# Edges laid out on 126 partitions instead of 128 in a two-layer graph kernel

## The chip, the cores and the metric

The kernel runs on one core of a Trainium2 chip. The time is device time in microseconds (us) of one execution; a kernel's time is the median of its executions. TensorE (PE), VectorE (DVE), ScalarE (ACT), GpSimd (POOL) and SyncE (SP) each run their own stream of instructions and meet at semaphores. 16 DMA engines move data between HBM and SBUF; plain transfers are asked for by SP, transfers whose rows are picked by a list of indices (indirect DMAs) by POOL.

## The reference

6,250 nodes with 256 features go through two layers; each has a graph part, a mixing part and a feed-forward part. The graph has 200,000 edges. `dst` is sorted, `src` is random, and every edge has 128 attributes. What the change touches is the first graph part and what the edges are prepared for:

```python
edge_index = jnp.stack([src, dst])
in_deg = jnp.minimum(jax.ops.segment_sum(ones, dst, num_segments=num_nodes), MAX_IN_DEGREE - 1)
out_deg = jnp.minimum(jax.ops.segment_sum(ones, src, num_segments=num_nodes), MAX_OUT_DEGREE - 1)
edge_proj = edge_attr @ W_sum + b_sum
sum3d = jax.ops.segment_sum(edge_proj, src, num_segments=num_nodes)
return x + z_in[in_deg] + z_out[out_deg] + cent_term + vor_term + sum3d
```

The second layer's graph part gathers `x[src]` and sums it by `dst`. So the edge attributes have to be brought together by `src`, and the pairs (src, dst) are wanted by `dst`.

## The kernel before, in words

Nodes are taken in 50 blocks (`NT`) of 125 (`P`). The block of an edge is `hi`, its place in the block is `lo`. Edges lie on `Q` = 128 partitions: partition p holds the `EF` = 1562 consecutive edges from p * EF on, in `EF` columns, and the `TAIL` = 64 edges that are left lie one on a partition in column EF. Columns are filled up to `EC` = 1568, a multiple of 32; the other slots hold pads. Every DVE and ACT instruction on edges works on [Q, EC], or on [Q, n columns].

The program is a row of blocks with a barrier after each.

**The first block** (lines 302 to 441). SP loads `src` and `dst`, DVE makes `hi` and `lo` (lines 400 to 407), and then the edges of each of the 50 blocks are counted: DVE counts the first 20 (`count_block`, line 200), ACT gets the other 30 from 31 sums of signs (line 427). Short matmuls (lines 253 to 263) turn the counts into the first place of every partition's edges of each block (`first_src`).

**The second block** (lines 463 to 893) holds the scatter. Columns go in halves of `HC` = 16. SP loads the attributes of a half, [128 partitions x 16 columns x 128 numbers], into one of the two halves of `ring` (`load`, line 535) as soon as the scatters of 16 columns out of that half have landed. POOL prepares a half with two small copies (`stage_half`, lines 568 and 569: the key into `ring`, the places into `stage`), and then issues one indirect DMA for each column (`scatter_half`, line 576): each takes one row of 516 bytes from each of the Q partitions and writes it to its place in `rows_by_src`. The two copies for the next half stand before the last three scatters of a half. There are EF + 1 scatters, 1563.

The places come from `rank_chunk` on DVE, for four chunks of columns (`CHUNKS`, in units of 32 columns: 0 to 6, 6 to 20, 20 to 34, 34 to EC/32). In each, the 50 blocks pass through a mask (line 621), a scan (627) and a predicated copy (634). POOL waits for the first chunk before its first scatter, and for each later one before it prepares that chunk's first half (`next_chunk`). After the ranks DVE counts `dst` in the same way (line 200, 50 instructions), and then makes one-hot tiles of 8 columns for `src` and then for `dst` (lines 605 and 608, EC/8 tiles for each), from which PE counts degrees (line 808). Layer statistics, the sigmoid terms and the attention-like mixing follow on DVE, ACT and PE; they need nothing of the scatter.

**After it** a short block writes `pairs_by_dst` in one direct copy, since `dst` is sorted; the next block (from line 1004 on) reads `rows_by_src` in windows of 1024 rows, and the rest of the program does not depend on Q.

Of the kernel before, what the change touches and what calls it, by code (L numbers as in the profile page):

```python
# [22 lines left out]
N, D, E, ED = 6250, 256, 200000, 128  # L23
P = 125
NT = N // P
Q = 128
EF = E // Q
TAIL = E - Q * EF
EC = -(-(EF + 1) // 32) * 32
# [57 lines left out]
def program(nc, a, out):  # L87
# [102 lines left out]
    def sort_dve(dve, ch, tools, hi, width, tab_b, tab_s, first2, base=None, signs=None):  # L190

        mask, cnt, tot, first, col, col_i, cum, row, win_f, ps, counted, summed = tools
        shift = width.bit_length() - 1
        nw = tab_b.shape[1]
        block_counted = sem("block_counted")

        def count_block(b, u):
            if not isinstance(b, int) or b >= 2:
                at(dve, block_counted, b - 1, passed["dve"])
            dve.tensor_scalar(mask[:, u * EC:(u + 1) * EC], hi[:], iota_f[:, bass.ds(b, 1)], 0.0,  # L200
                              ALU.is_equal, ALU.add, accum_out=cnt[:, bass.ds(b, 1)]).then_inc(block_counted, 1)

        for b in range(2):
            count_block(b, b)
        counted_here = SIGN_FROM if signs else NT
        with dve.Fori(1, counted_here // 2) as i:
            for u in range(2):
                count_block(i * 2 + u, u)
        dve.wait_ge(block_counted, counted_here)
        if signs:  # L210
            sums, signs_summed = signs
            rest = cnt[:, SIGN_FROM:NT]
            dve.wait_ge(signs_summed, NT + 1 - SIGN_FROM)
            ch.step(dve.tensor_tensor(rest, sums[:, SIGN_FROM:NT], sums[:, SIGN_FROM + 1:NT + 1], ALU.subtract))
            ch.step(dve.tensor_scalar(rest, rest, 0.5, None, ALU.mult))
        ch.step(dve.tensor_copy(tot[:], cnt[:]))
        dve.sem_inc(counted)
        dve.wait_ge(summed, 1)

        ch.step(dve.tensor_copy(tot[:], ps[:, 0, 64:64 + NT]))  # L220
        ch.step(dve.tensor_tensor_scan(first[:], tot[:], tot[:], 0.0, ALU.add, ALU.bypass))
        ch.step(dve.tensor_tensor(first2[:], first[:], tot[:], ALU.subtract))
        ch.step(dve.tensor_tensor(first[:], first2[:], ps[:, 0, 0:NT], ALU.add))
        ch.step(dve.tensor_scalar(first2[:], first[:], -1.0, None, ALU.add))

        ch.step(dve.tensor_copy(col[0:NT, 0:1], ps[0:NT, 0, 128:129]))
        ch.step(dve.tensor_scalar(col_i[0:NT, 0:1], col[0:NT, 0:1], float(width - 1), None, ALU.add))
        ch.step(dve.tensor_scalar(col_i[0:NT, 1:2], col_i[0:NT, 0:1], shift, None, ALU.arith_shift_right))
        ch.step(dve.tensor_copy(col[0:NT, 1:2], col_i[0:NT, 1:2]))
        ch.step(dve.scalar_tensor_tensor(out=col[0:NT, 2:3], in0=col[0:NT, 1:2], scalar=-float(width),  # L230
                                         in1=col[0:NT, 0:1], op0=ALU.mult, op1=ALU.add))
        dve.sem_inc(counted)
        dve.wait_ge(summed, 2)
        ch.step(dve.tensor_copy(col[0:NT, 3:4], ps[0:NT, 0, 129:130]))
        ch.step(dve.tensor_scalar(cum[0:NT, 0:nw], win_f[0:NT, 0:nw], col[0:NT, 3:4], None, ALU.is_ge))
# [12 lines left out]
    def sort_pe(pe, tools, nw):  # L248
# [1 line left out]
        mask, cnt, tot, first, col, col_i, cum, row, win_f, ps, counted, summed = tools  # L250
        h = nw // 2
        pe.wait_ge(counted, 1)
        pe.matmul(ps[:, 0, 0:NT], lower[:], cnt[:], start=True, stop=True)  # L253
        pe.matmul(ps[:, 0, 64:64 + NT], ones[:], cnt[:], start=True, stop=True)
        pe.matmul(ps[0:NT, 0, 128:129], cnt[:], ones[:, 0:1], start=True, stop=True).then_inc(summed, 1)
        pe.wait_ge(counted, 2)
        pe.matmul(ps[0:NT, 0, 129:130], lower[0:NT, 0:NT], col[0:NT, 1:2], start=True, stop=False)
        pe.matmul(ps[0:NT, 0, 129:130], ident[0:NT, 0:NT], col[0:NT, 1:2], start=False, stop=True).then_inc(summed, 1)
# [7 lines left out]
    def rank_edges(dve, ch, hi, before, mask, rank, pos_f, pos):  # L266

        with dve.Fori(0, NT // 2) as i:
            ch.enter(i, 6)
            for u in range(2):  # L270
                b = i * 2 + u
                m = mask[:, u * EC:(u + 1) * EC]
                ch.step(dve.tensor_scalar(m, hi[:], iota_f[:, bass.ds(b, 1)], None, ALU.is_equal))
                ch.step(dve.tensor_tensor_scan(rank[:], m, m, before[:, bass.ds(b, 1)], ALU.add, ALU.bypass))
                ch.step(dve.copy_predicated(pos_f[:], m.bitcast(U16), rank[:]))
            ch.leave(NT // 2)
# [10 lines left out]
    win1_base = sbuf(s12, "win1_base", [128, NW1])  # L287
    z_idx = sbuf(s12, "z_idx", [128, NT * 2], I32)
    win_f = XT[:, 4 * EC:4 * EC + NW2]
    pos_f = XT[:, 2 * EC:3 * EC]  # L290
    s01 = ExitStack()
    pair = sbuf(s01, "pair", [Q, EC * 2], I32)
    pos_src = sbuf(s01, "pos_src", [Q, EC], I32)
# [8 lines left out]
    with ExitStack() as ctx:  # L302
        src_i = sbuf(ctx, "src_i", [Q, EC], I32)
        dst_i = sbuf(ctx, "dst_i", [Q, EC], I32)
        src_f = XT[:, 0 * EC:1 * EC]
        dst_f = XT[:, 1 * EC:2 * EC]
        rank = XT[:, 3 * EC:4 * EC]
        mask = sbuf(ctx, "mask", [Q, 2 * EC], BF16)
        signs = sbuf(ctx, "signs", [Q, 2 * EC], BF16)
        sign_sums = sbuf(ctx, "sign_sums", [Q, 64])  # L310
# [110 lines left out]
        def _(act):  # L421
            act.wait_ge(hi_ready, 1)

            def sum_signs(b, u):
                if not isinstance(b, int) or b >= SIGN_FROM + 2:
                    at(act, signs_summed, b - SIGN_FROM - 1, passed["act"])
                act.activation(signs[:, u * EC:(u + 1) * EC], hi_src[:], ACT.Sign, bias=above[:, bass.ds(b, 1)],
                               accum_out=sign_sums[:, bass.ds(b, 1)]).then_inc(signs_summed, 1)

            for u in range(2):  # L430
# [6 lines left out]
        @block.tensor  # L437
        def _(pe):
            pe.wait_ge(falls_ready, 1)
            pe.matmul(ps[0:1, 3, 0:1], falls[:, 3:4], ones[:, 0:1], start=True, stop=True).then_inc(falls_summed, 1)  # L440
            sort_pe(pe, src_tools, NW1)


# [25 lines left out]
    with ExitStack() as ctx:  # L469
# [28 lines left out]
        pqkv = psum(ctx, "pqkv", 4)  # L498
        pq, pkv = pqkv[:, 0:2, :], pqkv[:, 2:4, :]

        dst_tools = (XT[:, 5 * EC:6 * EC].bitcast(BF16), sbuf(ctx, "d_cnt", [Q, NT]), sbuf(ctx, "d_tot", [Q, NT]),
                     sbuf(ctx, "d_first", [Q, NT]), sbuf(ctx, "d_col", [64, 8]), sbuf(ctx, "d_col_i", [64, 2], I32),
                     XT[:, 0:NW2], XT[0:1, NW2:2 * NW2], win_f, pqkv, sem("d_counted"), sem("d_summed"))
        ptr = psum(ctx, "ptr", 2)
# [1 line left out]
        phist = psum(ctx, "phist", 1)  # L506
        numbers = pctx[:, 0, 0:128]
        CHUNKS = ((0, 6), (6, 20), (20, 34), (34, EC // (2 * HC)))
        masks = XT[:, 6 * EC:7 * EC].bitcast(BF16).rearrange("p (m c) -> p m c", m=4)

        weights_in, mix_w_in, v_ones = sem("weights_in"), sem("mix_w_in"), sem("v_ones")
        ring_in = [sem("ring_in0"), sem("ring_in1")]
# [85 lines left out]
        def _(dve):  # L598
            ch = chain("dve", dve)

            def onehots(lo, hi, which):
                def body(t, u, i):
                    if later(t) or which:
                        at(dve, counted_to, t - 1 + which * (EC // 8), passed["dve"])
                    dve.tensor_tensor(lo1[:, u * 8 * P:(u + 1) * 8 * P].rearrange("p (c n) -> p c n", c=8),  # L605
                                      numbers[:, 0:P].unsqueeze(1).to_broadcast([Q, 8, P]),
                                      lo[:, bass.ds(t * 8, 8)].unsqueeze(2).to_broadcast([Q, 8, P]), ALU.is_equal)
                    dve.tensor_tensor(hi1[:, u * 8 * NT:(u + 1) * 8 * NT].rearrange("p (c n) -> p c n", c=8),  # L608
                                      numbers[:, 0:NT].unsqueeze(1).to_broadcast([Q, 8, NT]),
                                      hi[:, bass.ds(t * 8, 8)].unsqueeze(2).to_broadcast([Q, 8, NT]), ALU.is_equal).then_inc(onehot_ready, 1)  # L610
                tiles(dve, body, n=EC // 8)

            def rank_chunk(k):
# [16 lines left out]
                def place_block(b, u):  # L630
                    at(dve, scanned, b + (base + 1), passed["dve"])
                    if not isinstance(b, int) or base + b > 0:
                        at(dve, placed, b + base, passed["dve"])
                    dve.copy_predicated(out, masks[:, u, 0:n].bitcast(U16), pqkv[:, u, 0:n]).then_inc(placed, 1)
                    dve.tensor_copy(first_src[:, bass.ds(b, 1)], pqkv[:, u, n - 1:n]).then_inc(carried, 1)

                def block(b, u):
                    if not isinstance(b, int) or b < NT - 2:
# [262 lines left out]
    with s01, ExitStack() as ctx:  # L901
        pos_dst = sbuf(ctx, "pos_dst", [Q, EC], I32)
        mask = sbuf(ctx, "mask2", [Q, 2 * EC], BF16)
        rank, pos_f = XT[:, 0:EC], XT[:, EC:2 * EC]
        stage = sbuf(ctx, "stage2", [Q, 2 * 8], I32)
        pstage = sbuf(ctx, "pstage", [Q, 2 * 16], I32)
        pair_out = [sem("pair_out0"), sem("pair_out1")]
# [1445 lines left out]
```

## Time and profile before

| | us |
|---|---|
| median of 3 runs | 9076.64 (9044.06 to 9086.92) |
| the profiled execution, its own time | 9050.52 |
| its span | 9048.8 |

| engine | busy us of the span |
|---|---|
| PE | 3955.3 |
| PE weight loads | 3030.6 |
| DVE | 3517.7 |
| ACT | 719.5 |
| POOL | 3686.9 |

No engine is busy for half of the span, because the program is a row of stages with a different engine in front in each. A table by stretches of time says more than the totals: it shows in which stretch an engine works, and what the others do meanwhile. The rows are in the section before the prediction. Times of day are us from the start of the span. "issue" in a row is idle time for which the profile shows no other engine; "remote" is idle time that ended by a semaphore event that the profile can't put down to an instruction.

### The profile page before, as it was taken

Reading aid. Unit: us, or ns where it says so; the run is one execution under the profiler, and the core shown is the slowest. Engines: PE = TensorE matmul, PEld = TensorE weight load, DVE = VectorE, ACT = ScalarE, POOL = GpSimd, SP = SyncE. Lnnn points to the kernel's source line nnn. Section 1 sums busy time; section 2 is a strip of 40 time slices with the busy share of each in tenths; the row PEclk is TensorE's granted clock in tenths of the full one; section 3 lists DMA queues with packets and bytes.
Section 4 is the critical chain, followed back from the end, with each engine's and each line's share of the span. In section 5 each row is a group of like instructions: output and inputs, shape, how many; then the busy total and the mean of one; then the engine's idle time right before and its main releaser. Section 6 shows DMA issues by size and latency. Waiting matters only on the chain. (4 is left out here: it accounts for less than half of the span.)

```text
span 9048.8 us, 90350 instructions
## 1 busy us (share of the span) xinstructions
PE 3955.3 (44%) x18034; PEld 3030.6 (33%) x18035; DVE 3517.7 (39%) x7213; ACT 719.5 (8%) x1718; POOL 3686.9 (41%) x3922
## 2 busy tenths in 40 slices
PE   0000000000366366299378455565555555642792
PEld 0000000000355254199267233333333334432672
DVE  6321213200599722488622233333333333354112
ACT  2000000000000222000112000000000000221220
POOL 3576676677200000083000466666666663003104
PEclk9999999999999997599689566666667666875896
DMA  3233333333100000098000233333333334011113
GB/s 96 74 94 93 93 94 93 93 97 96 32 0 0 0 0 0 0 325 307 24 0 2 79 87 87 90 89 86 91 85 87 87 89 52 4 42 46 65 63 103
DMA packets 382516, 666.41 MB, mean 74 GB/s; under 512 B 207747, under 2 KB 236119, under 8 KB 369799
## 3 DMA queue, kind: packets, MB, share of 16 engines
q0 software_dynamic: 148768, 375.57, 14.0%
q1 hardware_dynamic: 233703, 290.37, 11.0%
q8 instruction: 13, 0.21, 0.0%
q14 instruction: 32, 0.26, 0.0%
HBM read 519.41 MB, written 146.21 MB: 74 GB/s over the span
## 5 line engine op out<-in xcount | busy, mean ns | idle before, releaser
L1496 POOL DMA_INDIRECT rows<-xn_rows,pw_in x1664 | 1624.2, 976 | 886.1 <-issue 484.7
L1629 PE MATMUL pg<-rows,hot 128*125 128x256 f32 x3328 | 1278.0, 536 | 1146.0 <-issue 401.1
L576 POOL DMA_INDIRECT rows_by_src<-ring,stage x1563 | 1499.7, 960 | 656.7 <-issue 488.8
L1629 PEld LDWEIGHTS pg<-rows,hot 128*125 128x125 f32 x3328 | 818.9, 265 | 1593.5 <-issue 1456.2
L1514 DVE TENSOR_TENSOR agg<-agg,pg 125x256 f32 x832 | 348.2, 419 | 1247.8 <-remote 544.2
L808 PE MATMUL phist<-hi,lo 128*125 128x50 bf16 x3136 | 413.6, 281 | 867.0 <-DVE hi L608 573.5
L253 PE MATMUL pqkv<-d_cnt,lower 128*128 128x50 f32 x2 | 0.7, 435 | 1578.5 <-remote 1578.5
L808 PEld LDWEIGHTS phist<-hi,lo 128*125 128x125 bf16 x3136 | 370.3, 222 | 911.6 <-issue 904.7
L1004 POOL MEMSET acc<- 128x6375 f32 x1 | 5.4, 5410 | 1493.0 <-POOLq L99 1493.0
L253 PEld LDWEIGHTS pqkv<-d_cnt,lower 128*128 128x128 f32 x2 | 0.5, 310 | 1579.0 <-remote 1579.0
L1095 PE MATMUL pw<-hot,win 128*128 128x125 f32 x3968 | 454.2, 277 | 164.1 <-DVE hot L1048 162.7
L1095 PEld LDWEIGHTS pw<-hot,win 128*128 128x128 f32 x3968 | 449.1, 193 | 169.8 <-issue 168.8
L1555 DVE TENSOR_TENSOR hot<-ids,pw_in 128x250 f32<-128x250 int32 x832 | 344.6, 414 | 385.9 <-issue 355.7
L605 DVE TENSOR_TENSOR lo<-pctx,lo_src 128x1000 bf16<-128x1000 f32 x196 | 232.8, 1188 | 629.3 <-remote 506.8
L627 DVE TENSOR_TENSOR_SCAN pqkv<-XT,first_src,pctx 128x448 f32<-128x448 bf16 (+2 forms) x200 | 206.9, 1034 | 485.6 <-issue 485.4
L1048 DVE SCALAR_TENSOR_TENSOR hot<-win,win_base,iota_f 128x1000 f32<-128x1000 f32 x248 | 338.5, 1365 | 26.1 <-POOL acc L1004 17.1
L964 POOL IOTA ids<- 128x6375 int16 x1 | 5.5, 5453 | 702.4 <-POOLq L1372 702.4
L183 ACT ACTIVATE rstd<-rstd 125x50 f32<-125x50 f32 x5 | 1.2, 245 | 3010.6 <-DVE rstd L176 3010.6
L605 DVE TENSOR_TENSOR lo<-pctx,lo_dst 128x1000 bf16<-128x1000 f32 x196 | 233.9, 1193 | 0.0
L2251 PE MATMUL e_py<-e_w,XT 128*128 x896 | 208.1, 385 | 45.1 <-ACT XT L2237 45.1
L2013 POOL MEMSET XT<- 32x12800 f32 x1 | 10.8, 10759 | 524.6 <-POOLq L99 524.6
L2198 POOL DMA_DIRECT2D moe_results<-XT x56 | 34.1, 610 | 456.1 <-DVE XT L2214 456.1
(413 smaller groups left out, 6424.6 us busy)
## 6 DMA issues: line engine op xcount, KB each, us to landing
win<-rows_by_src SPq DMA_DIRECT2D x248, 516.0 KB
ring<-in_edge_attr SPq DMA_DIRECT2D x97, 1024.0 KB
rows<-xn_rows,pw_in POOLq DMA_INDIRECT x1664
rows_by_src<-ring,stage POOLq DMA_INDIRECT x1563
XT<-moe_rows SPq DMA_DIRECT2D x56, 256.0 KB
moe_results<-XT POOLq DMA_DIRECT2D x56, 256.0 KB, 2.3
pw_in<-pairs_by_dst SPq DMA_DIRECT2D x832, 2.0 KB
e_w<-in_L_ffn_W SPq DMA_DIRECT2D x16, 512.0 KB
```

What stands on the lines that cost most here:

```text
L576: pool.indirect_dma_start(rows_d, bass.IndirectOffsetOnAxis(ap=stage[:, h * HC + j:h * HC + j + 1].bitcast(U32), axis=0), ring4[:, h, j, : ...
L605: dve.tensor_tensor(lo1[:, u * 8 * P:(u + 1) * 8 * P].rearrange("p (c n) -> p c n", c=8), numbers[:, 0:P].unsqueeze(1).to_broadcast([Q, 8, ...
L627: dve.tensor_tensor_scan(pqkv[:, u, 0:n], masks[:, u, 0:n], pctx[:, 0, 0:n], first_src[:, bass.ds(b, 1)], ALU.add, ALU.bypass).then_inc(sc ...
L808: mm = pe.matmul(phist[0:P, 0, which * 64:which * 64 + NT], lo1[:, (u * 8 + j) * P:(u * 8 + j + 1) * P], hi1[:, (u * 8 + j) * NT:(u * 8 + ...
L1048: dve.scalar_tensor_tensor(out=hot[:, (s % 4) * R1 * P:(s % 4 + 1) * R1 * P].rearrange("p (r n) -> p r n", r=R1), in0=keys.unsqueeze(2).to ...
L1095: mm = pe.matmul(pw[:, s % 4, 0:P], win[:, s * RC + r * (ED + 1):s * RC + r * (ED + 1) + ED], hot[:, ((s % 4) * R1 + r) * P:((s % 4) * R1 ...
L1496: pool.indirect_dma_start(rows[:, (2 * (s % RU) + r) * D:(2 * (s % RU) + r + 1) * D], None, xn2_d, bass.IndirectOffsetOnAxis(ap=pw_in[:, s ...
L1514: dve.tensor_tensor(tile, tile, pg[0:P, bank, 0:D], ALU.add).then_inc(acc_done, 1)
L1555: dve.tensor_tensor(hot[:, (s % 4) * 2 * P:(s % 4 + 1) * 2 * P].rearrange("p (r n) -> p r n", r=2), ids[:, bass.ds(b[s + early] * P, P)].u ...
L1629: mm = pe.matmul(pg[0:P, s % 4, 0:D], hot[:, ((s % 4) * 2 + r) * P:((s % 4) * 2 + r + 1) * P], rows[:, (2 * (s % RU) + r) * D:(2 * (s % RU ...
L2198: pool.dma_start(moe_y_d[bass.ds(t * MW, MW), :].rearrange("(p r) c -> p (r c)", p=128), yw[:, u * 2 * D:(u + 1) * 2 * D]).then_inc(y_out[ ...
L2251: mm = pe.matmul(py[:, v, 0:D], hT[:, (u * NH + m) * MW + v * 128:(u * NH + m) * MW + (v + 1) * 128], w2[:, bass.ds((e * NH + m) * D, D)], ...
```

## The change

`Q` becomes 126. `EF` is then 1587, `TAIL` 38, `EC` 1600 and the number of pad columns 13 instead of 6. Partition p holds edges 1587p and on. Tables that were [128, ...] and are used beside edges are cut to their first 126 partitions. Nothing changes its place in the program, but some counts follow from Q:

| | before | after |
|---|---|---|
| indirect scatters (EF + 1) | 1563 of 128 rows | 1588 of 126 rows |
| halves (of 16 columns, the last one shorter) | 98 | 100 |
| columns in the last chunk of ranks | 480 | 512 |
| columns in an instruction over all edges | 1568 | 1600 |
| one-hot tiles, `src` and `dst` | 392 | 400 |

```diff
-Q = 128
+Q = 126
...
-            dve.tensor_scalar(mask[:, u * EC:(u + 1) * EC], hi[:], iota_f[:, bass.ds(b, 1)], 0.0,
+            dve.tensor_scalar(mask[:, u * EC:(u + 1) * EC], hi[:], iota_f[0:Q, bass.ds(b, 1)], 0.0,
...
-        pe.matmul(ps[:, 0, 0:NT], lower[:], cnt[:], start=True, stop=True)
-        pe.matmul(ps[:, 0, 64:64 + NT], ones[:], cnt[:], start=True, stop=True)
-        pe.matmul(ps[0:NT, 0, 128:129], cnt[:], ones[:, 0:1], start=True, stop=True).then_inc(summed, 1)
+        pe.matmul(ps[0:Q, 0, 0:NT], lower[0:Q, 0:Q], cnt[:], start=True, stop=True)
+        pe.matmul(ps[0:Q, 0, 64:64 + NT], ones[0:Q, 0:Q], cnt[:], start=True, stop=True)
+        pe.matmul(ps[0:NT, 0, 128:129], cnt[:], ones[0:Q, 0:1], start=True, stop=True).then_inc(summed, 1)
...
-    pos_f = XT[:, 2 * EC:3 * EC]
+    pos_f = XT[0:Q, 2 * EC:3 * EC]
...
-                                      numbers[:, 0:P].unsqueeze(1).to_broadcast([Q, 8, P]),
+                                      numbers[0:Q, 0:P].unsqueeze(1).to_broadcast([Q, 8, P]),
...
-                    dve.tensor_tensor_scan(pqkv[:, u, 0:n], masks[:, u, 0:n], pctx[:, 0, 0:n], first_src[:, bass.ds(b, 1)],
+                    dve.tensor_tensor_scan(pqkv[0:Q, u, 0:n], masks[:, u, 0:n], pctx[0:Q, 0, 0:n], first_src[:, bass.ds(b, 1)],
```

The other edits of the diff cut `XT`, `iota_f`, `above`, `ones`, `numbers` and `ps` to 0:Q in the same way.

## Rows read from the trace of the kernel before

**Rows 1.** The page: totals of engines, busy tenths in 40 slices, chain that ended last.

```profile
PE 3955.3 (44%) x18034; PEld 3030.6 (33%) x18035; DVE 3517.7 (39%) x7213; ACT 719.5 (8%) x1718; POOL 3686.9 (41%) x3922
...
DVE  6321213200599722488622233333333333354112
...
POOL 3576676677200000083000466666666663003104
...
issue 1%; DVEq 0%; POOL 0%; DVE 0%; DMA 0%; PEldq 0%
```

**Rows 2.** Stretches of time: busy us (and instructions) of each engine, clock, DMA share.

```profile
core 0: us, PE busy (x) PEld busy (x) DVE busy (x) ACT busy (x) POOL busy (x), PEclk, DMA share, GB/s
...
1750.00:2000.00 250.00, 13.26 (x104) 12.05 (x104) 21.83 (x26) 0.00 (x0) 172.37 (x199) 1.00 0.31 93
...
2370.00:2500.00 130.00, 83.46 (x657) 75.84 (x657) 130.00 (x165) 0.00 (x0) 0.00 (x0) 1.00 0.00 0
```

**Rows 3.** Groups of POOL instructions, start to 2370 us: busy, mean ns | idle before.

```profile
L576 POOL DMA_INDIRECT rows_by_src<-ring,stage x1563 | 1499.7, 960 | 656.7 <-issue 488.8 <-remote 165.7 <-POOL stage L569 1.8
...
L568 POOL CAST ring<-pair 128x16 f32<-128x16 int32 x7 | 1.8, 257 | 100.5 <-DVE pos_src L656 100.5
```

**Rows 4.** POOL in order of time: start, duration, operation, idle before. Two halves.

```profile
602.88 0.96 POOL L576 DMA_INDIRECT rows_by_src<-ring,stage  x1 [0.31 <-issue]
604.14 0.96 POOL L576 DMA_INDIRECT rows_by_src<-ring,stage  x1 [0.30 <-issue]
605.10 0.23 POOL L568 CAST ring<-pair 128x16 f32 x1
605.24 0.20 POOL L569 COPY stage<-pos_src 128x16 int32 x1
605.61 0.98 POOL L576 DMA_INDIRECT rows_by_src<-ring,stage  x1 [0.16 <-issue]
606.89 0.95 POOL L576 DMA_INDIRECT rows_by_src<-ring,stage  x1 [0.30 <-issue]
608.14 0.96 POOL L576 DMA_INDIRECT rows_by_src<-ring,stage  x1 [0.30 <-issue]
615.07 0.96 POOL L576 DMA_INDIRECT rows_by_src<-ring,stage  x1 [5.96 <-remote]
```

**Rows 5.** POOL before chunk 1 of the ranks, in order of time.

```profile
384.22 0.96 POOL L576 DMA_INDIRECT rows_by_src<-ring,stage  x1 [0.30 <-issue]
433.03 0.36 POOL L568 CAST ring<-pair 128x16 f32<-128x16 int32 x1 [47.84 <-DVE pos_src L656]
```

**Rows 6.** Groups of POOL's DMAs in the whole span, shapes apart.

```profile
L1496 POOL DMA_INDIRECT rows<-xn_rows,pw_in x1664 | 1624.2, 976 | 886.1 <-issue 484.7 <-remote 152.2 <-PE pg L1629 146.8
...
L2022 POOL DMA_INDIRECT moe_rows<-XT,e_pos_x x100 | 98.0, 980 | 176.1 <-DVEq L2104 145.9 <-issue 30.2
...
L2198 POOL DMA_DIRECT2D moe_results<-XT x56 | 34.1, 610 | 456.1 <-DVE XT L2214 456.1
```

**Rows 7.** DMA queues from 600 to 2300 us (packets, MB, share), and issues.

```profile
q1 hardware_dynamic: 10800, 78.65, 16.7%
q0 software_dynamic: 38624, 79.80, 14.7%
...
ring<-in_edge_attr SPq DMA_DIRECT2D x75, 1024.0 KB
rows_by_src<-ring,stage POOLq DMA_INDIRECT x1208
```

**Rows 8.** Line 605: duration min/median/max, first and last start.

```profile
L605 DVE TENSOR_TENSOR lo<-pctx,lo_src x196: 1185/1185/1200, 1677.9 to 2619.9; 128x1000 bf16<-128x1000 f32 x196
L605 DVE TENSOR_TENSOR lo<-pctx,lo_dst x196: 1185/1190/1200, 2621.5 to 2937.3; 128x1000 bf16<-128x1000 f32 x196
```

**Rows 9.** DVE in order of time as the scatter ends.

```profile
2367.53 1.20 DVE L605 TENSOR_TENSOR lo<-pctx,lo_src 128x1000 bf16<-128x1000 f32 x1 [17.24 <-remote]
2368.64 0.56 DVE L608 TENSOR_TENSOR hi<-pctx,hi_src 128x400 bf16<-128x400 f32 x1
2369.12 1.19 DVE L605 TENSOR_TENSOR lo<-pctx,lo_src 128x1000 bf16<-128x1000 f32 x1
```

**Rows 10.** Groups of all engines, 120 to 2370 us.

```profile
L605 DVE TENSOR_TENSOR lo<-pctx,lo_src 128x1000 bf16<-128x1000 f32 x38 | 45.5, 1199 | 629.3 <-remote 506.8 <-issue 122.5
```

**Rows 11.** Groups of all engines from the start to 147 us.

```profile
L427 ACT ACTIVATE signs<-hi_src,above 128x1568 bf16<-128x1568 bf16 x31 | 49.1, 1588 | 10.7 <-DVEq L406 10.7
...
L200 DVE TENSOR_SCALAR_CACHE_REDUCE mask<-hi_src,iota_f 128x1568 bf16<-128x1568 bf16 x20 | 35.4, 1844 | 0.0
```

More of the change, by code:

```diff
@@ L218, in sort_dve @@
         dve.wait_ge(summed, 1)
-        ch.step(dve.tensor_copy(tot[:], ps[:, 0, 64:64 + NT]))
+        ch.step(dve.tensor_copy(tot[:], ps[0:Q, 0, 64:64 + NT]))
         ch.step(dve.tensor_tensor_scan(first[:], tot[:], tot[:], 0.0, ALU.add, ALU.bypass))
         ch.step(dve.tensor_tensor(first2[:], first[:], tot[:], ALU.subtract))
-        ch.step(dve.tensor_tensor(first[:], first2[:], ps[:, 0, 0:NT], ALU.add))
+        ch.step(dve.tensor_tensor(first[:], first2[:], ps[0:Q, 0, 0:NT], ALU.add))
         ch.step(dve.tensor_scalar(first2[:], first[:], -1.0, None, ALU.add))
@@ L272, in rank_edges @@
                 m = mask[:, u * EC:(u + 1) * EC]
-                ch.step(dve.tensor_scalar(m, hi[:], iota_f[:, bass.ds(b, 1)], None, ALU.is_equal))
+                ch.step(dve.tensor_scalar(m, hi[:], iota_f[0:Q, bass.ds(b, 1)], None, ALU.is_equal))
                 ch.step(dve.tensor_tensor_scan(rank[:], m, m, before[:, bass.ds(b, 1)], ALU.add, ALU.bypass))
@@ L304, in program @@
         dst_i = sbuf(ctx, "dst_i", [Q, EC], I32)
-        src_f = XT[:, 0 * EC:1 * EC]
-        dst_f = XT[:, 1 * EC:2 * EC]
-        rank = XT[:, 3 * EC:4 * EC]
+        src_f = XT[0:Q, 0 * EC:1 * EC]
+        dst_f = XT[0:Q, 1 * EC:2 * EC]
+        rank = XT[0:Q, 3 * EC:4 * EC]
         mask = sbuf(ctx, "mask", [Q, 2 * EC], BF16)
@@ L426, in sum_signs @@
                     at(act, signs_summed, b - SIGN_FROM - 1, passed["act"])
-                act.activation(signs[:, u * EC:(u + 1) * EC], hi_src[:], ACT.Sign, bias=above[:, bass.ds(b, 1)],
+                act.activation(signs[:, u * EC:(u + 1) * EC], hi_src[:], ACT.Sign, bias=above[0:Q, bass.ds(b, 1)],
                                accum_out=sign_sums[:, bass.ds(b, 1)]).then_inc(signs_summed, 1)
@@ L439, in _ @@
             pe.wait_ge(falls_ready, 1)
-            pe.matmul(ps[0:1, 3, 0:1], falls[:, 3:4], ones[:, 0:1], start=True, stop=True).then_inc(falls_summed, 1)
+            pe.matmul(ps[0:1, 3, 0:1], falls[:, 3:4], ones[0:Q, 0:1], start=True, stop=True).then_inc(falls_summed, 1)
             sort_pe(pe, src_tools, NW1)
@@ L499, in program @@
         pq, pkv = pqkv[:, 0:2, :], pqkv[:, 2:4, :]
-        dst_tools = (XT[:, 5 * EC:6 * EC].bitcast(BF16), sbuf(ctx, "d_cnt", [Q, NT]), sbuf(ctx, "d_tot", [Q, NT]),
+        dst_tools = (XT[0:Q, 5 * EC:6 * EC].bitcast(BF16), sbuf(ctx, "d_cnt", [Q, NT]), sbuf(ctx, "d_tot", [Q, NT]),
                      sbuf(ctx, "d_first", [Q, NT]), sbuf(ctx, "d_col", [64, 8]), sbuf(ctx, "d_col_i", [64, 2], I32),
@@ L508, in program @@
         CHUNKS = ((0, 6), (6, 20), (20, 34), (34, EC // (2 * HC)))
-        masks = XT[:, 6 * EC:7 * EC].bitcast(BF16).rearrange("p (m c) -> p m c", m=4)
+        masks = XT[0:Q, 6 * EC:7 * EC].bitcast(BF16).rearrange("p (m c) -> p m c", m=4)
         weights_in, mix_w_in, v_ones = sem("weights_in"), sem("mix_w_in"), sem("v_ones")
@@ L605, in body @@
                     dve.tensor_tensor(lo1[:, u * 8 * P:(u + 1) * 8 * P].rearrange("p (c n) -> p c n", c=8),
-                                      numbers[:, 0:P].unsqueeze(1).to_broadcast([Q, 8, P]),
+                                      numbers[0:Q, 0:P].unsqueeze(1).to_broadcast([Q, 8, P]),
                                       lo[:, bass.ds(t * 8, 8)].unsqueeze(2).to_broadcast([Q, 8, P]), ALU.is_equal)
                     dve.tensor_tensor(hi1[:, u * 8 * NT:(u + 1) * 8 * NT].rearrange("p (c n) -> p c n", c=8),
-                                      numbers[:, 0:NT].unsqueeze(1).to_broadcast([Q, 8, NT]),
+                                      numbers[0:Q, 0:NT].unsqueeze(1).to_broadcast([Q, 8, NT]),
                                       hi[:, bass.ds(t * 8, 8)].unsqueeze(2).to_broadcast([Q, 8, NT]), ALU.is_equal).then_inc(onehot_ready, 1)
@@ L620, in mask_block @@
                         at(dve, placed, b + (base - 3), passed["dve"])
-                    dve.tensor_scalar(masks[:, u, 0:n], hi_src[:, lo:lo + n], iota_f[:, bass.ds(b, 1)], None, ALU.is_equal).then_inc(masked, 1)
+                    dve.tensor_scalar(masks[:, u, 0:n], hi_src[:, lo:lo + n], iota_f[0:Q, bass.ds(b, 1)], None, ALU.is_equal).then_inc(masked, 1)
                 def scan_block(b, u):
@@ L633, in place_block @@
                         at(dve, placed, b + base, passed["dve"])
-                    dve.copy_predicated(out, masks[:, u, 0:n].bitcast(U16), pqkv[:, u, 0:n]).then_inc(placed, 1)
-                    dve.tensor_copy(first_src[:, bass.ds(b, 1)], pqkv[:, u, n - 1:n]).then_inc(carried, 1)
+                    dve.copy_predicated(out, masks[:, u, 0:n].bitcast(U16), pqkv[0:Q, u, 0:n]).then_inc(placed, 1)
+                    dve.tensor_copy(first_src[:, bass.ds(b, 1)], pqkv[0:Q, u, n - 1:n]).then_inc(carried, 1)
                 def block(b, u):
@@ L903, in program @@
         mask = sbuf(ctx, "mask2", [Q, 2 * EC], BF16)
-        rank, pos_f = XT[:, 0:EC], XT[:, EC:2 * EC]
+        rank, pos_f = XT[0:Q, 0:EC], XT[0:Q, EC:2 * EC]
         stage = sbuf(ctx, "stage2", [Q, 2 * 8], I32)
```

## The prediction

> **What bounds the kernel now.** I read the page first, only for its shape. No engine is busy for half of the span, and the chain that ended last names nothing above 1% [rows 1], so it says nothing of the part that the change touches. The busy tenths do: in slices 2 to 10 POOL is high and DVE low, in slices 12 to 14 DVE is full and POOL idle [rows 1]. The table of stretches makes this plain: from 1750 to 2000 us POOL is busy for 172 of 250 us and DVE for 22, and from 2370 us on DVE is busy for all of 130 us with POOL at none [rows 2]. So this part is two stages one after the other, first POOL's scatters, then DVE's one-hot tiles.
>
> In the first, POOL issues 1563 scatters [rows 3]. They start 1.26 us apart: 0.96 us busy and 0.30 us of issue [rows 4]. 1563 x 1.262 = 1972 us of some 2240 (from 127 us to 2363). Most of the rest is two things. 100.5 us are waits for ranks [rows 3]; 47.84 of them fall into the stage, before chunk 1, and end at 433 us [rows 5], the others lie ahead of the first scatter. 165.7 us are gaps named "remote" [rows 3]; I counted 40 of them, which stand between two halves, as the one of 5.96 us does in [rows 4].
>
> DVE's one-hots for `src` begin while the scatter still runs, at 1677.9 us [rows 8], but get through 38 tiles only until 2370, against 629 us of idle time before them [rows 10]. That is one in 18.2 us (from 1677.9 to 2367.5 by 38), about one in a half of scatters. As soon as POOL is through, the tiles follow each other 1.6 us apart [rows 9]; from 2621.5 to 2937.3 us 195 steps give 1.62 us a tile [rows 8]. So the end of the scatter sets the start of the fast tiles, and everything later waits for these. A microsecond more on POOL after 433 us is a microsecond of the kernel's time.
>
> The transfers are not the limit. From 600 to 2300 us the loads of `ring` take 16.7% of the 16 engines and the scatters 14.7% [rows 7].
>
> **The change part by part.** All sums are against the profiled execution, 9050.5 us, and then moved to the median of the runs, 9076.6, which stands 26 us above it.
>
> *25 more scatters.* At 1.262 us [rows 4] they cost 31.6 us, if one of 126 rows has the price of one of 128. The trace has no indirect DMA with other than 128 rows, so this price is the open point. What it has: a gather of 1024-byte rows (960 to 980 ns, lines 1496 and 2022) costs what a scatter of 516-byte rows does (960 ns), and a direct copy takes 610 ns [rows 3, 6]. So bytes do not count, and about 0.35 us go into what an indirect one has and a direct one has not. If all of the 1.262 us went with the rows, 126 would cost 1.242. The 0.020 us saved count on the 1399 scatters after 433 us only, since before that the ranks of chunk 1 set the time [rows 5]; that gives 28 us back. The bounds of this case are thus +3.6 and +31.6. I take +31.6, as each row of the trace has one price whatever it moves, and keep the other end for the range.
>
> *Two more halves.* 165.7 us of gaps over 98 halves are 1.7 us each [rows 3]: +3.4. The two copies of a half lengthen one step from 1.26 to 1.47 us (604.14 to 605.61) [rows 4]: +0.4. The ranks of the last chunk work on 512 instead of 480 columns; they are off the path, since POOL waited in the trace for chunks 0 and 1 alone (two releases by line 656, and 47.84 us of 100.5 for the second) [rows 3, 5]. Without this cover it would be 50 scans, masks and copies at a fifteenth more.
>
> *Eight more one-hot tiles.* At 1.62 us 13.0 us. The scatter is some 35 us longer and lets two more through at one in 18.2 us. Six are left on the path: +9.8. PE's matmuls for them lie under DVE.
>
> *Longer instructions in the first block.* 1600 for 1568 columns is 2.04% more. ACT's 31 sums at 1588 ns [rows 11] give +1.0, and DVE's conversions before them +0.4; the 20 counts on DVE (35.4 us, [rows 11]) lie beside ACT's. Together +1.4. The 50 counts of `dst` lie under the scatter.
>
> *Loads.* A load of `ring` keeps each of the 16 engines busy for 0.167 x 1700 / 75 = 3.8 us [rows 7]. The next one has 20 us, a half of scatters, so even an eighth more hides. If it didn't, 100 x 0.5 would be 50 us. The first loads and the pairs are under 1 us: taken as 0.
>
> Everything after the second block has the same counts: 0. The sum is 31.6 + 3.4 + 0.4 + 9.8 + 1.4 = **+46.6 us**; 9097 for the profiled execution, **9123** for the median. With the cheap end of the scatter it is +18.6, 9095.
>
> **The rivals.** What decides is how POOL's work depends on the number of rows. The packets say how a scatter is dealt out now: 38624 by 1208 is 32, two for each of 16 engines, so 8 rows an engine; a load has 10800 / 75 = 144 packets, 9 for each of 16 [rows 7]. 126 is no multiple of 16. Dealt out evenly it goes over 14 engines with 9 rows each.
>
> The Trainium skill ("DMA: Bandwidth & Descriptors", the section on why a DMA increments its semaphore by 16) says just this: the number of engines is the largest one up to 16 that divides the slowest dimension, 14 here. It adds that some direct copies issued by POOL use all 16 with the count rounded up, which would leave 8 rows an engine and the case above. The packets of the trace agree with 16 engines for 128 rows; no run so far shows 126.
>
> *A: fewer engines, less work for POOL (faster).* If POOL's time goes with the engines that it serves, 14 for 16 takes an eighth off: off 0.61 us (the part that a direct copy has too) 0.076, off all of 0.96 us 0.12. On 1399 scatters that is 106 to 168 us, less the 46.6 above: -60 to -121, in the middle -90, 8986. For it: a direct copy of 256 KB costs 610 ns whatever its bytes [rows 6]. Against it: no row tells work by engine from work by row.
>
> *B: more rows an engine, more work for POOL (slower).* If POOL writes one row's descriptors for all engines in one step, the steps go from 8 to 9. The same parts then grow by an eighth: +0.076 to +0.12 us, 106 to 168 us on 1399 scatters, with the 46.6: +153 to +215, in the middle +184, 9261. It decides against my forecast as soon as the step between two scatters is over 1.27 us. For and against it stands the same as for A. Here the rule of the skill and the forecast part: by 14 engines, A or B holds; by 16 with the count rounded up, neither.
>
> *C: the layout does not reach the path.* If the gaps between halves grew smaller with less on the DMA engines, or the tiles found more room beside POOL, the 15 us apart from the scatters would go: +20 to +30, inside the forecast's range.
>
> **How the numbers follow.** The forecast with its two ends (9090 to 9130) 0.42, C 0.03, A 0.30, B 0.25. Over 0.5% is 45 us, about what a measurement of this kernel can tell from no change. The forecast's upper end lies right on it: I give 0.23 of its 0.42 to within 0.5%, and 0.19 to slower. C is within. A is faster but for 0.02, B is slower. Faster 0.28, same 0.28, slower 0.44. A gives 8956 to 9017 and B 9230 to 9292; the range of 8970 to 9270 leaves the outer quarter of A and the outer third of B out, together under 0.2. The forecast's own is 9085 to 9135.
>
> **What would show it.** In the trace of the changed kernel: the step between two scatters (1.26 by the forecast, 1.14 to 1.19 by A, 1.34 to 1.38 by B), with 1588 of them; the last at some 2400 us, by A at 2260, by B at 2535. The packets of a scatter, 32 or 28, and of a load, 144 or 140, tell over how many engines they go. 400 tiles at 1.62 us, some 360 of them after the last scatter. The gaps between halves at some 170 us in sum. The wait before chunk 1 should end at about 435 us. I am wrong if the step is another, if the gaps change by more than 30 us, or if POOL begins to wait for loads or for chunks 2 and 3.

## The result, and the profile after

The changed kernel takes 9119.36 us (median of 5 runs, 9111.91 to 9128.71) against 9069.5 us (9044.06 to 9086.92) for the kernel before beside it: ratio 1.0061, 95% interval 1.0049 to 1.0074, some 55 us slower by the ratio (the two medians are 50 us apart). The forecast was 9123.

POOL's instructions of line 576 in the changed kernel: count, ns min/median/max, first and last start, and what ended its idle time. [rows 3, 4] have the same of before.

```profile
L576 POOL DMA_INDIRECT rows_by_src<-ring,stage x1588: 980/984/1185, 128.8 to 2388.9; - x199
its engine sat idle before it (us, times) until:
  issue: 481.1, 1537
  remote: 140.2, 34
```

In order of time, the scatters come 1.29 us apart (642.88 to 644.17), not 1.26:

```profile
642.88 0.98 POOL L576 DMA_INDIRECT rows_by_src<-ring,stage  x1 [0.30 <-issue]
644.17 0.98 POOL L576 DMA_INDIRECT rows_by_src<-ring,stage  x1 [0.30 <-issue]
```

The one-hots, against [rows 8]: 400 instead of 392, the last at 2977.9 instead of 2937.3 us.

```profile
L605 DVE TENSOR_TENSOR lo<-pctx,lo_src x200: 1187/1219/1269, 1733.3 to 2654.0; 126x1000 bf16<-126x1000 f32 x100
L605 DVE TENSOR_TENSOR lo<-pctx,lo_dst x200: 1186/1198/1267, 2655.6 to 2977.9; 126x1000 bf16<-126x1000 f32 x100
```

The queues from 600 to 2300 us, against [rows 7]: 154280 / 76 = 2030 packets a load where there were 144, and 58176 / 1213 = 48 a scatter where there were 32. The prediction had 32 or 28. By their sizes in the trace, the 32 are 16 packets of 4128 bytes (8 rows of 516) and 16 of 4 bytes; the 48 are 14 of 4128 bytes and 14 of 516, with 20 of 4 or 32 bytes. This fits 14 engines with 8 + 1 rows each (the trace does not name the engine of a packet).

```profile
q0 software_dynamic: 58176, 78.96, 16.6%
q1 hardware_dynamic: 154280, 78.45, 16.4%
...
ring<-in_edge_attr SPq DMA_DIRECT2D x76, 1008.0 KB
rows_by_src<-ring,stage POOLq DMA_INDIRECT x1213
```

The block that follows (first instruction of line 1004) starts at 3891.7 us:

```profile
L1004 POOL MEMSET acc<- x1: 5410/5410/5410, 3891.7 to 3891.7; 128x6375 f32 x1
```

### The profile page after: what moved, and what is told of

Same layout as the page of the kernel before. It is cut to its first block and busy times, and to the rows that moved or that the text cites. A ratio compares the mean times of both kernels' runs of the same rounds, so it can differ in the third digit from the quotient of the medians.

```text
span 9127.0 us, 90610 instructions
## 1 busy us (share of the span) xinstructions
PE 3924.1 (43%) x18098; PEld 3019.6 (33%) x18099; DVE 3541.7 (39%) x7229; ACT 720.3 (8%) x1718; POOL 3731.0 (41%) x3951
## 3 DMA queue, kind: packets, MB, share of 16 engines
q0 software_dynamic: 174976, 375.70, 14.5%
## 5 line engine op out<-in xcount | busy, mean ns | idle before, releaser
L1496 POOL DMA_INDIRECT rows<-xn_rows,pw_in x1664 | 1603.3, 964 | 960.1 <-issue 482.7
L576 POOL DMA_INDIRECT rows_by_src<-ring,stage x1588 | 1564.7, 985 | 625.1 <-issue 481.1
L808 PE MATMUL phist<-hi,lo 126*125 126x50 bf16 x3200 | 422.2, 281 | 828.6 <-DVE hi L608 429.8
L808 PEld LDWEIGHTS phist<-hi,lo 126*125 126x125 bf16 x3200 | 378.0, 222 | 874.2 <-issue 867.1
L605 DVE TENSOR_TENSOR lo<-pctx,lo_src 126x1000 bf16<-126x1000 f32 x200 | 245.2, 1226 | 602.0 <-remote 418.1
L627 DVE TENSOR_TENSOR_SCAN pqkv<-XT,first_src,pctx 126x448 f32<-126x448 bf16 (+2 forms) x200 | 210.5, 1052 | 510.6 <-issue 510.4
L605 DVE TENSOR_TENSOR lo<-pctx,lo_dst 126x1000 bf16<-126x1000 f32 x200 | 239.3, 1196 | 0.0
```

Source lines behind the costliest of these rows:

```text
L576: pool.indirect_dma_start(rows_d, bass.IndirectOffsetOnAxis(ap=stage[:, h * HC + j:h * HC + j + 1].bitcast(U32), axis=0), ring4[:, h, j, : ...
L627: dve.tensor_tensor_scan(pqkv[0:Q, u, 0:n], masks[:, u, 0:n], pctx[0:Q, 0, 0:n], first_src[:, bass.ds(b, 1)], ALU.add, ALU.bypass).then_in ...
L808: mm = pe.matmul(phist[0:P, 0, which * 64:which * 64 + NT], lo1[:, (u * 8 + j) * P:(u * 8 + j + 1) * P], hi1[:, (u * 8 + j) * NT:(u * 8 + ...
L1496: pool.indirect_dma_start(rows[:, (2 * (s % RU) + r) * D:(2 * (s % RU) + r + 1) * D], None, xn2_d, bass.IndirectOffsetOnAxis(ap=pw_in[:, s ...
```

## The experiments

**Is the difference of the profiles the difference of the kernels?** The two profiled executions differ by 78 us, more than the medians. Only 35 us of it had come by the start of line 1004 (3856.3 in the first profile of before), and the gather stage (line 1496) was 53 us longer. So I took the kernel before again, and once with its tables in HBM made as large as in the changed kernel:

```diff
-    rows_d = nc.dram_tensor("rows_by_src", (E + W1 + Q * EPAD, ED + 1), F32, kind="Internal").ap()
-    pairs_d = nc.dram_tensor("pairs_by_dst", (E + W1 + Q * EPAD, 2), I32, kind="Internal").ap()
+    rows_d = nc.dram_tensor("rows_by_src", (E + W1 + 126 * 13, ED + 1), F32, kind="Internal").ap()
+    pairs_d = nc.dram_tensor("pairs_by_dst", (E + W1 + 126 * 13, 2), I32, kind="Internal").ap()
```

> The kernel before once more, unchanged, for a second profile. From the start to the last scatter 2362 +- 10 us, the gaps between halves 166 +- 20 us in sum. If the 53 us by which the gather stage (line 1496, first to last start, 2509 us in the first profile, 2562 in that of the changed kernel) differed come from chance, this profile has another value in between or beyond; if they come from the change, it has 2509 +- 10.

> The kernel before, with the two tables in HBM (rows by source, pairs by destination) made as large as in the changed kernel, which moves the tables behind them to other addresses; nothing else. If addresses are behind the longer gather stage, its 2509 us go to about 2560 and the ratio is 1.003 to 1.006. If not, 2509 to 2520 us and a ratio of 1.000 +- 0.001.

Measured: ratios 0.9999 (0.9987 to 1.0011) and 1.0000 (0.9988 to 1.0012). The gather stage took 2525 us in the first and 2504 us in the second, after 2509 in the first profile. Addresses are not behind it. The stage spreads by some 20 us between executions of one kernel; that the changed kernel's 2562 us is all chance is not shown, but nothing that the change touches runs there, and on the other kind of chip (below) the stage takes 2137 us in the changed kernel and 2141 to 2144 us in four kernels on 128 partitions. Up to line 1004, where the change acts, before has 3856.3, 3844.9 and 3847.7 us, and the changed kernel 3891.7: +42 us on their mean. The interval of the ratio reaches down to 44 us; what lies between 42 and 55 us comes after line 1004 or is noise, and was not tracked down.

**The rows alone.** The changed kernel with fewer edges, so that all counts are those of before and only the 126 rows are left of the change:

```diff
-N, D, E, ED = 6250, 256, 200000, 128
+N, D, E, ED = 6250, 256, 196876, 128
...
-NW2 = -(-((E + NT * (W2 - 1)) // W2) // 4) * 4
+NW2 = -(-((200000 + NT * (W2 - 1)) // W2) // 4) * 4
```

> The changed kernel with 196876 edges (the last 3124 are left out), so that 126 partitions give 1562 columns, a tail of 64, 1563 scatters, 1568 columns and 392 one-hot tiles, all as in the kernel before; only the 126 rows of a DMA are left of the change. Theory (one scatter of 126 rows costs 0.026 us more): 1374 scatters after chunk 1 of the ranks at +0.026 give +36 us on the last scatter, less what the gaps between halves gave back in the changed kernel (25 us), so the time is 10 to 36 us over that of before, ratio 1.001 to 1.004. Rival (the loss comes from the counts, 25 scatters and 8 tiles, and the price does not matter): ratio 1.000. The gather stage has fewer edges and may be some us shorter, so the start of the stage after the second block (3856 us before, 3892 after) is the better measure: 3866 to 3892 by the theory, 3856 by the rival.

Measured: ratio 0.9998 (0.9986 to 1.0010). The profile of this kernel, line 576:

```profile
L576 POOL DMA_INDIRECT rows_by_src<-ring,stage x1563: 983/987/1386, 127.9 to 2343.7; - x196
its engine sat idle before it (us, times) until:
  issue: 471.7, 1510
  remote: 129.8, 35
```

And of the kernel before, taken again on the same chip:

```profile
L576 POOL DMA_INDIRECT rows_by_src<-ring,stage x1563: 952/958/1235, 127.4 to 2360.9; - x196
its engine sat idle before it (us, times) until:
  issue: 486.0, 1514
  remote: 165.7, 41
```

Each scatter is 29 ns longer, and yet the last one starts 17 us earlier, and line 1004 at 3836.8 us against 3844.9 and 3847.7 in the two profiles of before on this chip. I had expected 3866 to 3892 us, the price less the gains; they cancel, and a little more. The theory missed, and the number is nearer to the rival's. So on this chip 126 rows for themselves cost nothing in sum, by one profile and with 3124 edges fewer, and the loss is that of the counts. But it is not true, as the rival had it, that the price does not matter: it is there, and something else is given back. Reading the starts of all scatters after chunk 1 of the ranks one by one gives what. A long step is one that is over the usual one by more than 0.6 us; the sums are what is over it, in us:

| | before, three profiles | same counts, 126 rows | changed kernel |
|---|---|---|---|
| usual step | 1.26 to 1.27 | 1.29 | 1.29 |
| chunk 1 ready, first scatter after it | 436 to 438 | 429 | 433 |
| long gaps between halves, count and sum | 38: 135 to 147 | 33: 119 | 35: 133 |
| long steps inside a half, count and sum | 15 to 17: 25 to 27 | 4: 5 | 3: 2 |

The steps inside a half are clearly apart. The gaps between halves are less so: one profile of before has 135 us and the changed kernel 133.

**The price by the number of rows.** A kernel of its own with sets of 32 scatters:

> A kernel of its own that leaves the whole reference out: it copies x to the output, loads tiles of 128, 126, 120 and 112 partitions x 16 columns x 512 bytes from SP, then issues on POOL, with DVE idle, 32 scatters of 516-byte rows each for 128, 126, 125, 124, 120, 112, 96, 64 and again 128 rows, and 32 gathers each of 1024-byte rows for 128, 126 and 112 rows. Theory (the price goes with the rows that one DMA engine gets, on as many engines up to 16 as divide the row count evenly): steps of 1.26 us at 128 (8 rows on 16 engines), 1.29 at 126 (9 on 14), 1.26 at 120 (8 on 15), 1.24 at 112 (7 on 16), and clearly more, 1.6 us or above, at 125 (25 on 5). Rival 1 (a fixed extra for any count that is not a multiple of 16): 1.29 at 126, 125, 124 and 120 alike, 1.26 or less at 112. Rival 2 (price by rows in all): it falls steadily from 128 to 64 and 126 lies under 128. For the loads, if packets go by the engine count alone, 144 packets a load at 128 and 140 at 126.

The lines are those of its sets, in the order of the text; ns min/median/max, first and last start:

```profile
L59 POOL DMA_INDIRECT rows_scratch<-ring,idx x32: 957/962/1148, 211.9 to 251.3; - x32
L62 POOL DMA_INDIRECT rows_scratch<-ring,idx x32: 972/977/987, 257.9 to 297.6; - x32
L65 POOL DMA_INDIRECT rows_scratch<-ring,idx x32: 1175/1180/1184, 300.4 to 346.4; - x32
L68 POOL DMA_INDIRECT rows_scratch<-ring,idx x32: 1306/1311/1320, 350.1 to 403.1; - x32
L71 POOL DMA_INDIRECT rows_scratch<-ring,idx x32: 982/989/997, 407.1 to 447.2; - x32
L74 POOL DMA_INDIRECT rows_scratch<-ring,idx x32: 930/938/947, 449.9 to 488.4; - x32
L77 POOL DMA_INDIRECT rows_scratch<-ring,idx x32: 907/912/926, 490.9 to 528.7; - x32
L80 POOL DMA_INDIRECT rows_scratch<-ring,idx x32: 896/900/911, 531.2 to 568.5; - x32
L83 POOL DMA_INDIRECT rows_scratch<-ring,idx x32: 957/962/977, 571.5 to 610.7; - x32
L89 POOL DMA_INDIRECT got<-in_x,gidx x32: 945/949/993, 613.9 to 652.8; - x32
L96 POOL DMA_INDIRECT got<-in_x,gidx x32: 986/995/1010, 657.3 to 697.5; - x32
L103 POOL DMA_INDIRECT got<-in_x,gidx x32: 926/927/937, 701.1 to 739.4; - x32
```

Of the scatters (lines 59 to 83), 128 rows cost 962 ns, 126 cost 977, 125 cost 1180, 124 cost 1311, 120 cost 989, 112, 96 and 64 cost 938, 912 and 900. The steps are 0.30 us longer: 1.27 and 1.28 for 128 and 126, 1.29 for 120. Two things can be read off. Between the multiples of 16, the time falls by 24 to 26 ns for each row less that an engine of 16 gets (8, 7, 6 rows), and by 12 ns for the two rows from 6 to 4. And 120 rows cost 27 ns more than 128, although the packets of a scatter (15 of 4128 bytes) give each of 15 engines the same 8 rows. At 125 and 124 the packets fit 25 rows on 5 engines and 31 on 4, and these cost most. But the two do not add up to the price of 126: one row more for an engine and the extra of 120 would be 962 + 25 + 27 = 1014 ns, and it is 977. My first theory had 1.29 us for 126 (1.28 measured) and missed 120 (1.29, not 1.26), rival 1 missed 125, rival 2 missed 126. So no rule of the three gives the price of 126 rows, and it is not the same everywhere: 15 ns over 128 in this kernel, 26 to 29 in the big one, and 46 for a gather of 1024-byte rows (949 at 128, 995 at 126, 927 at 112; lines 89, 96 and 103). Why is open. The loads of this kernel show the engines too: 12180 packets for 6 loads of 126 partitions are 126 x 16 + 14 each, 864 for 128 partitions are 128 + 16 each.

```profile
q1 hardware_dynamic: 12180, 6.19, 59.7%
...
q1 hardware_dynamic: 864, 6.29, 63.3%
```

(From stretches of 6 loads each, 93.3 to 129.3 us and 56 to 93 us.) At 128 partitions a packet holds the 8 KB of a partition, at 126 one row of 512 bytes, and the load is not slower for it: 60% of the engines over the same time.

**Loads and DVE as the cause of the gaps.** The gaps between halves seemed to shrink with 126 rows. Theory G: they come from the big packets of a load; H: from POOL and DVE taking turns. Four kernels, all on 128 partitions: loads cut in two at partition 112 or at 64, loads of one column, and one-hots that wait for the last scatter.

```diff
-                sp.dma_start(ring4[:, h, 0:n, 0:ED], attr[:, bass.ds((2 * i + h) * HC, n), :]).then_inc(ring_in[h], 16)
+                sp.dma_start(ring4[0:112, h, 0:n, 0:ED], attr[0:112, bass.ds((2 * i + h) * HC, n), :]).then_inc(ring_in[h], 16)
+                sp.dma_start(ring4[112:Q, h, 0:n, 0:ED], attr[112:Q, bass.ds((2 * i + h) * HC, n), :]).then_inc(ring_in[h], 16)
```

```diff
+            for h in range(2):
+                dve.wait_ge(ring_out[h], 16 * (HC * LOOPS + LAST[h]))
             onehots(lo_src, hi_src, 0)
```

> The kernel before (128 partitions), with each load of a half of ring cut into one of partitions 0 to 111 and one of 112 to 127. In the price table a load of 112 partitions went in 512-byte packets (1808 packets) and one of 128 in 8-KB packets (144), so here most of the bytes go in small packets, as in the changed kernel, while the scatters stay at 128 rows and 1.262 us. Theory G (the gaps between halves are POOL held up by the big packets of a load, and shrink with small ones): the gaps after chunk 1 of the ranks fall from about 198 us in sum to 150 to 165, the last scatter goes from 2361 to 2315 to 2335 us, ratio 0.994 to 0.998. Rival H (the gaps come from POOL and DVE taking turns and depend on POOL's step alone): sum 190 to 205 us, ratio 1.000.

> Control for the split of the loads: the kernel before with each load cut into partitions 0 to 63 and 64 to 127, both powers of two, so I expect 8-KB packets as before (some 160 a load) and one more transfer issued by SP. By theory G and by rival H alike: gaps 190 to 205 us in sum, ratio 1.000 +- 0.001. If it is as fast as the split into 112 and 16, the number of transfers and not the packets is the cause.

> The kernel before, but every load of ring after the first two brings one column of the 16, so most attributes are stale and the sums by source are wrong; same semaphores, a sixteenth of the bytes. By theory G the gaps between halves almost vanish: sum after chunk 1 from 198 to under 60 us, last scatter at 2220 us or earlier, ratio about 0.985. By rival H they stay, 190 to 205 us, ratio 1.000.

> The kernel before, but DVE waits for the last scatter before it begins its one-hot tiles, so from about 1660 us on DVE does nothing beside POOL. It costs the 36 tiles that ran beside the scatters: 36 x 1.61 = +58 us. By theory G the gaps go on as before from 1660 to 2362 (about 70 us), last scatter at 2361 +- 8, ratio about 1.006. By rival H they vanish there: last scatter at 2295 +- 10 us, one-hots end at about the same time as before, ratio 0.999 to 1.000.

All four fell on a chip on which the kernel before itself takes 6990.88 us (6984.82 to 7001.22), not 9030. The ratios there: 0.9999 (0.9990 to 1.0008), 1.0000 (0.9991 to 1.0009), 0.9996 (0.9986 to 1.0005) and 1.2147 (1.2128 to 1.2165). The kernel with loads cut at 64, on this chip, lines 577 and 606 (576 and 605 of before):

```profile
L577 POOL DMA_INDIRECT rows_by_src<-ring,stage x1563: 952/958/1232, 127.6 to 2162.8; - x196
its engine sat idle before it (us, times) until:
  issue: 464.7, 1457
  POOL stage L570: 16.9, 98
...
L606 DVE TENSOR_TENSOR lo<-pctx,lo_src x196: 1185/1185/1199, 524.1 to 833.7; 128x1000 bf16<-128x1000 f32 x196
L606 DVE TENSOR_TENSOR lo<-pctx,lo_dst x196: 1185/1190/1200, 835.2 to 1151.0; 128x1000 bf16<-128x1000 f32 x196
```

There are no "remote" gaps, and DVE goes at full speed beside POOL: the one-hots are over at 1151 us and not at 2937. Everything else of the block lies under the scatters, and these alone set its length. So the loads, whether whole, cut or nearly empty, do nothing here, and the one-hots held back cost 1500 us. On G and H this says nothing, since the gaps are not there to be shrunk. It does show that gaps and a starved DVE come and go together with the chip. The kernel with the one-hots held back shows one thing more: its last scatter starts at 2143.1 us, some 20 us earlier than in the other three.

```profile
L576 POOL DMA_INDIRECT rows_by_src<-ring,stage x1563: 952/958/1235, 127.4 to 2143.1; - x196
```

So on this chip, too, what runs beside the scatters costs POOL a little, about 1% of the stage, though without any long gap.

**Both kernels on the other kind of chip.**

> The changed kernel, unchanged. The four runs before this one were on a chip on which the kernel before takes 6991 us and DVE works at full speed beside POOL's scatters, with no gaps between halves (POOL 127 to 2161 us, one-hots over at 1151 us). On such a chip POOL's scatters are the whole length of the second block, nothing is given back by shorter gaps, and the change costs 25 x 1.288 + 1563 x 0.026 = 73 us: ratio 1.0105, last scatter at 2235 us. On a chip like that of the first runs (before 9030 us): ratio 1.004 to 1.008, last scatter 2389 +- 10, gaps after chunk 1 of the ranks 150 to 165 us in sum against 198.

> The loads cut into 112 and 16 partitions once more, since the first try fell on a chip without gaps. On a chip with gaps: theory G (big packets of a load hold POOL up) gives gaps of 150 to 165 us in sum, last scatter 2315 to 2335 us and a ratio of 0.994 to 0.998; rival H (POOL and DVE taking turns) 185 to 200 us, last scatter 2355 to 2362, ratio 1.000. On a chip without gaps: 1.000, and nothing is learned.

> DVE waits for the last scatter before its one-hot tiles, once more. On a chip with gaps: by theory G the gaps go on after 1660 us, last scatter 2361 +- 8, ratio about 1.006; by rival H they vanish there, last scatter 2295 +- 10, ratio 0.999 to 1.000. On a chip without gaps 1.215 as before, since there the tiles and the mixing ran beside the scatters.

The chip was again one without gaps (before 6994.09 us). The changed kernel: 7039.14 us, ratio 1.0062 (1.0045 to 1.0079); the others 0.9997 (0.9988 to 1.0007) and 1.2143 (1.2122 to 1.2163). Whether G or H holds stays open. The first profile of before speaks against H as the whole story: in 11 of its 37 gaps of over 1 us no instruction of DVE runs. The changed kernel's line 576 here:

```profile
L576 POOL DMA_INDIRECT rows_by_src<-ring,stage x1588: 980/984/1236, 128.8 to 2212.5; - x199
```

The last scatter of the four 128-row kernels above that changed the loads alone starts at 2161.3 to 2166.2 us, 2164 in the mean. 48 us later is less than the 73 that I had added up from 25 scatters and the price. Most of what is missing are steps inside a half. In the kernel with loads cut at 64, the scatter after number 337 starts 2.82 us after it:

```profile
562.48 0.95 POOL L577 DMA_INDIRECT rows_by_src<-ring,stage  x1 [0.30 <-issue]
565.30 0.95 POOL L577 DMA_INDIRECT rows_by_src<-ring,stage  x1 [1.87 <-issue]
566.55 0.96 POOL L577 DMA_INDIRECT rows_by_src<-ring,stage  x1 [0.31 <-issue]
```

The same happens after scatters 113, 225, 337 and so on, once in exactly 112, 13 times, in every profile with 128 rows on either kind of chip (with 1.56 to 1.94 us of extra each), and never in one with 126. Then 25 x 1.29 + 1563 x 0.026 - 13 x 1.56 = 32.3 + 40.6 - 20.3 = 52.6 us, against 48 measured. Line 1004 starts at 2230.5 us, against 2185.0 to 2188.6 us in the four: 42 to 45 us later, which is all of the 45 us between the two times.

**Long rows of scatters.**

> A kernel of its own that leaves the whole reference out: x is copied to the output, then POOL issues, with DVE idle and no loads, seven sets of 400 scatters of 516-byte rows: 128, 112, 96, 64, 126, 120 and again 128 rows each. In the traces with 128 rows, on both kinds of chip, one step in 112 is 1.56 us longer (after scatters 113, 225, 337 ...), and with 126 rows none is. Theory R (a ring of descriptors for each DMA engine fills, 9 entries a scatter at 128 rows, 112 x 9 = 1008): a pause once in 112 at 128 rows, once in 126 at 112 rows (8 entries), in 144 at 96 (7), in 202 at 64 (5), and none as long at 126 and 120 rows, where fewer than 16 engines are used and the rings of the engines do not wrap together. Rival S (the pause belongs to the loop of the real kernel, its waits or its loads): no pause in any set. The steps apart from pauses should be 1.262 to 1.27 us at 128, 1.24 at 112, 1.22 at 96, 1.20 at 64, 1.28 at 126 and 1.29 at 120, as in the first table.

Around scatter 113 of the first set (128 rows, line 42) and scatter 102 of the set with 126 rows (line 54):

```profile
252.75 0.96 POOL L42 DMA_INDIRECT rows_scratch<-ring,idx  x1 [0.30 <-issue]
256.84 0.97 POOL L42 DMA_INDIRECT rows_scratch<-ring,idx  x1 [3.14 <-issue]
...
2418.90 1.09 POOL L54 DMA_INDIRECT rows_scratch<-ring,idx  x1 [0.30 <-issue]
2423.20 0.98 POOL L54 DMA_INDIRECT rows_scratch<-ring,idx  x1 [3.21 <-issue]
```

Pauses of 2.8 to 3.2 us beyond the step come once in 113 scatters at 128 rows, in 127 at 112, in 128 at 96 and at 64, in 102 at 126, and in 113 at 120. With one entry for each row that an engine gets and one more (9, 8, 10 and 9), 113, 127, 102 and 113 scatters are 1017, 1016, 1020 and 1017 entries. That fits one ring of some 1020 entries for each engine, and at 96 and 64 rows (896 and 640 entries) a limit of 128 scatters would have to come first; both are read off these periods, nothing else shows them. The price table fits: of its 32 scatters of 124 rows (31 rows and one entry more) the last one starts 3 us late, after 31 x 32 = 992 entries, and at 125 rows (832 entries) none does. S falls, since the pause comes without loops and loads. R as I had put it was right for 128 and 112 rows and missed the other four: the periods at 96 and 64, and above all that 126 and 120 rows have the pause too. In the kernel with 126 rows it is not there, and with 128 rows it is shorter (1.56 to 1.94 us), so that it is the same pause is not shown, and why the changed kernel is spared it stays open. From the middle of the second set on, the steps were 1.40 us for every count of rows, for 64 and for the last set of 128 alike, so this table gives no prices; that is open too.

## Why the prediction was right, and where it was lucky

The time (9123 forecast, 9119 measured), the direction and the stage were right; of the terms two were not, and that the time was met to 4 us is luck: the price of a scatter was missed by 36 us, pauses and gaps that were not forecast gave about as much back, and the median of before that the sum started from (9076.6) was 7 us above the one measured beside the changed kernel. On the first kind of chip, against the mean of three profiles of before:

| term | forecast, us | measured, us |
|---|---|---|
| 25 more scatters | +31.6 | +32.3 (25 x 1.29) |
| price of 126 rows | 0 to -28 | +36 (1374 x 0.026) |
| pauses once in 112 | not in it | -22 |
| gaps between halves | +3.4 | -10 (143 to 133) |
| chunk 1 ready | 0 | -4 |
| last scatter, in all | +35 | +29.5 (2359.4 to 2388.9) |
| tiles on the path | +9.8 | +14.6 |
| start of line 1004 | +46.6 | +42 |

The five measured terms above the last scatter add up to 32 us and not to 29.5; the rest are small differences between steps that I put down to no term.

*The price of a scatter* was the step that failed, and by the prediction's own sign ("I am wrong if the step is another"): 1.29 us and not 1.26. I took the step at 128 rows, 1.262 us, as the upper bound of the case and called everything above 1.27 rival B, at +0.076 to +0.12. The truth was +0.026, between the two and outside of both. Neither rival held: A had the engines right (14, by the sizes of the packets) but the sign wrong, B the sign but three to four times the size. The 26 ns are about what a row more or less for an engine costs between 6 and 8 rows (24 to 26 ns), but the price table has 15 ns for the same step from 128 to 126, so that this is the reason is not shown. A bound of "same price" is no upper bound where a new shape is dealt out in another way.

*The pauses and gaps* paid it back. The steps of [rows 4] were read from one stretch of two halves. A list of all steps would have shown the one of 2.8 to 3.2 us in every 112, which a table by groups hides in its 656.7 us of idle time [rows 3].

*The tiles.* I let 38 pass before the end of the scatter and two more for the longer stage. By the last scatter it was 36 before (40 in one of the three profiles) and 35 after, so 9 more were left: 9 x 1.61 = 14.5. The one in 18.2 us of [rows 8, 10] is no rate to add to.

*What held:* the end of the scatter and then the tiles set the time, the loads and the later chunks stayed under cover, 100 halves, and the wait before chunk 1 ended at 429 us. The rule of the Trainium skill ("DMA: Bandwidth & Descriptors", on why a DMA increments its semaphore by 16), by which 126 partitions go over 14 engines, is borne out by the loads (126 x 16 + 14 packets) and by the scatters (14 packets of 8 rows and 14 of one).

On the other kind of chip the same change costs 45 us of 6994: there the price counts on all 1563 scatters, the tiles on none, and of what was given back only the pauses are left.

## What to carry to other kernels

Fewer partitions for the same data mean more instructions and more DMAs, and an indirect DMA need not get cheaper with fewer rows. Of the counts tried here only multiples of 16 were cheaper than 128: 128 rows cost 962 ns, 112 cost 938, but 126 cost 977, 120 cost 989 and 124 cost 1311. Before costing a long row of equal instructions by one step, list all the steps and look for the rare long ones. And a share of time that one engine takes from another may belong to the chip: look at whether the ratio holds on a second one.

## What the hardware showed

- Two kinds of chips. The kernel before takes 9030 to 9070 us on one and 6991 to 6994 us on the other. On the first, DVE gets one tile in 17 to 19 us through beside POOL's scatters and POOL has 40 gaps of 4 us; on the second neither is so. Which chip a kernel gets decides over 2000 us, and a change over 50. Why is not known, and as each chip was seen in one sitting, that a chip keeps its kind is not shown either.
- A load of 512-byte pieces goes in 144 packets at 128 partitions and in 2030 at 126, and six such loads, one after the other, take some 35 us either way. It goes in small packets (2080) also when it is cut into 64 and 64 partitions, and these hold the engines longer: 27.1% of their time from 600 to 1100 us, against 17.9% for the changed kernel's loads on that kind of chip. The kernel's time is the same.
- A scatter of 126 rows goes in 14 packets of 8 rows and 14 of one row, one of 120 rows in 15 of 8 rows.
- In a long row of scatters POOL pauses for 2.8 to 3.2 us about once in 1016 to 1020 entries, if a scatter counts one for each row of an engine and one more, or once in 128 scatters.
